# Token-mixing layers in halves of one stream each, set against the FFN of the half before; masks of attn1 on VectorE

## The reference, cut to what matters

```python
def _L1_attn_ref(x, Wqkv, Wo):          # 16 heads of 16
    ...
    scores = jnp.einsum('bhqd,bhkd->bhqk', q, k) / math.sqrt(DH)
    causal = jnp.tril(jnp.ones((t, t), dtype=bool))
    scores = jnp.where(causal, scores, -jnp.inf)
    attn = jax.nn.softmax(scores, axis=-1)
    ...
def _layer(x, wqkv, qs, ksc, wo, lg, lb, w1, b1, w2, b2):   # 8 heads of 64, window 128
    h = shift_token(x)
    q, k, v = jnp.split(h @ wqkv, 3, axis=-1)
    ...
    q = l2norm(q) * qs
    k = l2norm(k) * ksc
    q, k = rotary_xpos(q, k)
    o = local_attention(q, k, v)
    ...
    x = x + o @ wo
    h = shift_token(x)
    ...                                  # layer norm, gain and bias
    h = h @ w1 + b1
    a, g = jnp.split(h, 2, axis=-1)
    h = a * jax.nn.gelu(g, approximate=False)
    x = x + h @ w2 + b2
    return x
x = x + _L1_attn_ref(_layernorm(x, axis=-1), L1_attn_Wqkv, L1_attn_Wo)
x = x + _L1_ffn_ref(_layernorm(x, axis=-1), ...)     # _layer twice
```

## Time and profile before

| what | value |
|---|---|
| median of 3 runs | 2722.84 us (2721.39 to 2726.86) |
| the profiled execution | 2726.97 us |
| its span, first to last instruction | 2725.2 us, 46487 instructions |
| mean granted clock of TensorE | 0.916 |
| attn1 | 598 to 1234 us |
| layers | 1234 to 2725 us |

### The profile page before, as it was taken

How to read it: one execution, slowest core, us unless ns; L and a number is a source line. 1 busy time by engine, 2 the same in 40 slices (tenths; PEclk the granted TensorE clock), 3 DMA queues, 4 the chain that set the end, 5 groups by cost and what they waited for, 6 DMA issues and landing times.

```text
span 2725.2 us, 46487 instructions
## 1 busy us (share of the span) xinstructions
PE 2377.3 (87%) x16770; PEld 1799.0 (66%) x16770; DVE 1564.7 (57%) x4242; ACT 1206.8 (44%) x3055; POOL 965.5 (35%) x1367
## 2 busy tenths in 40 slices
PE   7999699977888888886788898898888988988988
PEld 4666599965464555545567676686676766866766
DVE  5555422225647566546657558567675585585754
ACT  1112133324755555653624636437345354372362
POOL 2222122214443333323715416236155262462442
PEclk9999699987988879788899998998999989989999
DMA  3222311121010100003000000000010000000000
GB/s 123 93 100 97 106 38 36 39 71 32 3 58 7 47 18 33 2 10 111 2 16 16 17 16 1 17 16 33 16 57 16 26 8 32 16 2 32 16 2 32
DMA packets 75794, 96.31 MB, mean 35 GB/s; under 512 B 6141, under 2 KB 68946, under 8 KB 75314
## 3 DMA queue, kind: packets, MB, share of 16 engines
q1 hardware_dynamic: 70642, 81.72, 8.9%
q0 software_dynamic: 3408, 9.31, 1.2%
q10 hardware_dynamic: 1520, 2.31, 0.2%
HBM read 62.51 MB, written 30.28 MB: 34 GB/s over the span
## 4 chain that ended last, share of the span: by engine, by line
PE 30%; DVE 14%; POOL 4%; issue 3%; ACT 2%; DVEq 0%; POOLq 0%; ACTq 0%
PE l_bank L1977 6%; PE l_bank L1978 5%; PE l_bank L1979 5%; PE l_bank L2084 4%; POOL l_probs L1622 3%; DVE l_work L1699 3%; DVE l_ss L1680 2%; PE l_bank L2019 2%; PE l_turned L2037 2%; PE l_bank L2053 2%; DVE l_probs L1697 1%; DVE l_probs L1718 1%; PE l_turned L1977 1%; PE l_turned L1978 1%; PE l_turned L1979 1%
## 5 line engine op out<-in xcount | busy, mean ns | idle before, releaser
L1622 POOL TENSOR_SCALAR l_probs<-l_probs,l_rinv 128x256 f32<-128x256 f32 (+1 forms) x512 | 223.3, 455 | 129.0 <-DVE l_rinv L1723 127.9
L1058 DVE TENSOR_REDUCE c_cnmax<-cbank 128x1 f32<-128x384 f32 (+3 forms) x384 | 206.2, 595 | 108.5 <-PE cbank L1249 89.5
L1896 ACT ACTIVATE l_probs<-l_probs,l_nmax 128x256 f32<-128x256 f32 (+1 forms) x512 | 238.9, 473 | 0.0
L1158 ACT ACTIVATE c_cprobsT<-cbank 128x384 f32<-128x384 f32 (+1 forms) x384 | 180.5, 522 | 97.9 <-PE cbank L1275 97.1
L1718 DVE CUSTOM_DVE_ANT_0 l_probs<-l_bank,mask 128x256 f32<-128x256 f32 (+1 forms) x512 | 169.1, 387 | 37.3 <-PE l_bank L2019 22.8
L1606 POOL TENSOR_TENSOR l_work<-l_work 128x512 f32<-128x512 f32 x64 | 82.7, 1292 | 272.5 <-DVE l_work L1699 271.6
L979 POOL TENSOR_SCALAR_AFFINE_SELECT c_cprobsT<-c_cprobsT 128x256 f32<-128x256 f32 x256 | 99.4, 412 | 165.9 <-ACT c_cprobsT L1158 163.8
L2019 PE MATMUL l_bank<-l_kT,l_flipped 64*128 64x256 f32 (+1 forms) x1024 | 152.6, 420 | 0.0
L1942 ACT ACTIVATE l_v<-l_bank,l_b 128x512 f32<-128x512 f32 (+1 forms) x96 | 66.1, 689 | 193.0 <-PE l_bank L1979 193.0
L718 PE MATMUL h_bank<-m_xsT,m_w1s 128*128 128x128 f32 x1248 | 148.4, 278 | 0.3 <-issue 0.3
L1977 PE MATMUL l_bank<-l_part,l_w_high 128*128 128x512 f32 (+1 forms) x288 | 123.1, 427 | 26.3 <-DVE l_yT L1789 26.3
(11 more groups left out here) (273 smaller groups left out, 6358.5 us busy)
## 6 DMA issues: line engine op xcount, KB each, us to landing
w<-in_W1T SPq DMA_DIRECT2D x8, 1024.0 KB, 8.3
w<-in_W2T SPq DMA_DIRECT2D x8, 1024.0 KB, 11.3
l_came<-y_d SPq DMA_DIRECT2D x16, 512.0 KB, 4.2
ys_d<-m_y SPq DMA_DIRECT2D x39, 128.0 KB, 1.7
xn_d<-a_prods SPq DMA_DIRECT2D x8, 512.0 KB, 3.1
c_came<-x_d SPq DMA_DIRECT2D x8, 512.0 KB, 4.8
y_d<-c_raw SPq DMA_DIRECT2D x8, 512.0 KB, 3.7
y_d<-l_probs SPq DMA_DIRECT2D x8, 512.0 KB, 3.4
```

Source lines behind the costliest of these rows:

```text
L1058: dve.tensor_reduce(nmax[:, c % 2, qt, s, i:i + n], S, AX, ALU.max, negate=True).then_inc(nmax_ready[s], 1)
L1158: act.activation(probsT[s][:, c % 2, i, k0:k0 + w], turned_place(j, s)[:, 0:w], ACT.Exp).then_inc(probs_ready[s], 1)
L1622: pool.tensor_scalar(probs[s][:, held(u), h, 0:n], probs[s][:, held(u), h, 0:n], rinv[s][:, u, h:h + 1], 1.0, ALU.mult, ALU.mult)\
L1896: act.activation(probs[s][:, held(u), h, 0:n], probs[s][:, held(u), h, 0:n], ACT.Exp, bias=nmax[s][:, u, h:h + 1], scale=-1.0, accum_out=r ...
```

## The change

**attn1.** The setup block is gone: its DMAs, the row copies and gathers of POOL and the memsets of DVE stand at the head of the main block, with waits where the data is first used. The mask matmuls on PE are gone; DVE takes the row maximum with one tensor_tensor_reduce per head, which adds a bf16 table `later` (zero, and the mask for the diagonal block) on the way. It writes its unused full result to the last rows of `raw`, and waits for the reduction of the same stream before it.

**layers.** The setup block is gone too: w_qkv is cast and split in six pieces, of which a projection waits for its own; each late weight has its own load and semaphore. The trips are replaced by 16 halves n = 2 * pair + s, one stream each, all eight heads of a stream in eight steps of four heads' score blocks. The attention of half n is written together with the hidden products of half n - 1 (HIDDEN_AT gives them to the eleven slots of the attention), contract(n - 1) with the shift and norm of half n, flip_hn and its splits with the rotations of half n + 1. Probabilities have two buffers, FLIP_LAG is 2, OUT_LAG 3. The PSUM has two score banks, two turned banks, one output bank and three free banks, which q, k and v of the projections share with hidden products. Hidden sums are copied out raw (`take_out`, g by ACT, a by DVE); gelu and gated work from SBUF at the end of the slots, so that the table of ACT changes from exponential to gelu once a half. Gain and bias (L1783) go from DVE to ACT. POOL's bias rows stand in attention steps 1 to 4; the splits of w1 and w2 stand in the steps of the first half of layer one, and of the second and third half of layer two.

```diff
-                        S = score_place("scores", u, s)[:].rearrange("p (h k) -> p h k", h=n)[:, :, 0:(qt + 1) * P]
-                        dve.tensor_reduce(nmax[:, c % 2, qt, s, i:i + n], S, AX, ALU.max, negate=True).then_inc(nmax_ready[s], 1)
+                        wide = (qt + 1) * P
+                        ban = later[:, (NT - 1 - qt):NT, :].rearrange("p a b -> p (a b)")
+                        if pair * UNITS + u:
+                            dve.wait_ge(nmax_ready[s], pair * UNITS + u)
+                        for h in range(n):
+                            last = dve.tensor_tensor_reduce(raw[:, CHUNKS - NS + s, h * 2 * P:h * 2 * P + wide], score_place("scores", u, s)[:, h * 2 * P:h * 2 * P + wide], ban, -1.0, 3e38,
+                                                            ALU.add, ALU.min, nmax[:, c % 2, qt, s, i + h:i + h + 1])
+                        last.then_inc(nmax_ready[s], 1)
...
-                                pe.matmul(score_place("scores", u, s)[:, i * 2 * P:i * 2 * P + wide], qT[s][r, p, qt * P:(qt + 1) * P],
-                                          kT[s][r, p, 0:wide], start=True, stop=False)
-                            for half in range(2):
-                                for s in range(NS):
-                                    h = head(s, c, i0 + i)
-                                    r = slice(64 * (h % 2), 64 * (h % 2) + 64)
-                                    at = i * 2 * P + qt * P
-                                    last = pe.matmul(score_place("scores", u, s)[:, at:at + P], g.mask[r, 3 * half, :], g.mask[r, 3 * half + 2, :],
-                                                     start=False, stop=half == 1)
-                                    if half == 1 and i == n - 1:
-                                        last.then_inc(scores_ready[s], 1)
+                                last = pe.matmul(score_place("scores", u, s)[:, i * 2 * P:i * 2 * P + wide], qT[s][r, p, qt * P:(qt + 1) * P],
+                                                 kT[s][r, p, 0:wide], start=True, stop=True)
+                                if i == n - 1:
+                                    last.then_inc(scores_ready[s], 1)
 
                     def flip_maxima(c):
...
+                for s in range(NS):
+                    pool.tensor_copy(rowb[s][:], g.row_of[:, s * NT:(s + 1) * NT]).then_inc(row_first, 1)
+                pool.wait_ge(row_first, NS)
+                for s in range(NS):
+                    gather(pool, s, 0)
...
+        FLIP_LAG, OUT_LAG, SPAN = 2, 3, 11
+        HIDDEN_AT = ((0, 1), (2, 3), (4, 5), (6,), (7,), (8,), (9,), (10,), (11,), (), ())
...
+        probs = sb("probs", [P, 2, 2, 2, 2 * P])
+        probsT = sb("probsT", [P, 2, 2, 4, P])
...
+        score_bank = [ps(f"score{i}") for i in range(2)]
+        turned_banks = ctx.enter_context(nc.psum_tensor("l_turned", [P, 2, L], F32))
+        turned_bank = [turned_banks[:, a, :] for a in range(2)]
+        out_bank = ps("out")
+        free_bank = [ps(f"free{i}") for i in range(3)]
...
+                    for t in range(NT + 1):
+                        if t < NT:
+                            add(t, 0)
+                        if t:
+                            pool.wait_ge(added[s], pair * (2 * NT) + 2 * t)
+                            pool.wait_ge(inv_ready[s], pair * NT + t)
+                            normalise(pool, s, t - 1, 1).then_inc(k_rotated[s], 1)
+                        if t < NT:
+                            add(t, 1)
...
+                def rotations(n, between):
+                    project(n, 0)
+                    between()
+                    project(n, 1)
+                    flip_qk(n, 0)
+                    project(n, 2)
+                    flip_qk(n, 1)
+                    project(n, 3)
+
...
+                flip_rows(0)
+                rotations(0, lambda: None)
+                for n in range(HALVES + 1):
+                    att, ffn = n < HALVES, n > 0
+                    for p in range(SPAN):
+                        if att and p < 2:
+                            scores(n, p)
+                        if ffn:
+                            for k in HIDDEN_AT[p]:
+                                hidden(n - 1, k)
+                        if att and p < 2:
+                            flip_qk(n, p + 2)
+                        if p == 9 and n + 1 < HALVES:
+                            flip_rows(n + 1)
+                        if att and p >= 2:
+                            if p - FLIP_LAG < STEPS:
+                                flip(n, p - FLIP_LAG)
+                            if p < STEPS:
+                                scores(n, p)
+                            if 0 <= p - OUT_LAG < STEPS:
+                                output(n, p - OUT_LAG)
+                            if p == SPAN - 2:
+                                attended(n, 0)
+                                attended(n, 1)
+                    if att:
+                        attended(n, 2)
+                        attended(n, 3)
+                    if ffn:
+                        contract(n - 1, 0, 1)
+                    if att:
+                        shift(n)
+                    if ffn:
+                        contract(n - 1, 1, NT)
+                    if n + 1 < HALVES:
+                        rotations(n + 1, lambda: flip_hn(n))
+                    elif att:
+                        flip_hn(n)
         nc.all_engine_barrier(sems_to_clear=sem_range)
 
         with nc.Block() as block:
```

More of the change, by code:

```diff
@@ L1419, in phase_layers @@
+        gate = flipped
         kT = stream("kT", [P, HP2, L])
         v = stream("v", [P, NT, INNER])
[L1422 removed]
         hn = [a[:, 2:NT, :].rearrange("p a (b n) -> p (a b) n", n=D) for a in v]
[L1424 to L1430 removed]
@@ L2057, in hidden @@
-                    def hidden(s, c):
-                        if c >= 2:
-                            pe.wait_ge(u_done[s], pair * UC + c - 1)
-                        r = rows(c)
-                        for i in range(2):
-                            for k in range(DC):
-                                last = product(bank[s][2 * (c % 2) + i][0:r, :], [w1[a][:, k, i * HID + c * P:i * HID + c * P + r] for a in (1, 0)],
-                                               [a[:, k, 1:L + 1] for a in (part[s], yT[s])], k == 0, k == DC - 1)
-                        last.then_inc(ag_psum[s], 1)
@@ L2087, in _ @@
-                    for u in range(UNITS + OUT_LAG):
-                        if 0 <= u - FLIP_LAG < UNITS:
-                            flip(u - FLIP_LAG)
-                        if 2 <= u < UNITS:
-                            scores(u)
-                        if u >= OUT_LAG:
-                            output(u - OUT_LAG)
-                        if u == UNITS:
-                            pe.wait_ge(late_in, (layer + 1) * LATE_ALL)
-                        for s in range(NS):
-                            if u >= UNITS:
-                                attended(s, u - UNITS)
@@ new lines, in output @@
+                def output(n, j):
+                    s = place(n)[0]
+                    J = n * STEPS + j
+                    for a in range(2):
+                        pe.wait_ge(pT_ready[a], J + 1)
+                    if j == 0 and n:
+                        f, f_pair = place(n - 1)[0:2]
+                        pe.wait_ge(hn_ready[f], f_pair * (2 * NT) + 2 * NT)
+                    elif j and j % 2 == 0:
+                        pe.wait_ge(oT_ready, J // 2)
+                    cp, w = step_of(j)
+                    k0, width = (w - 1, 2) if w else (0, 1)
+                    for h in range(2):
+                        for k in range(width):
+                            for half in range(2):
+                                head, at = (2 * (2 * cp + h) + half) * DH2, (2 * (j % 2) + h) * P
+                                last = pe.matmul(out_bank[DH2 * half:DH2 * (half + 1), at:at + P], v[s][:, k0 + k, head:head + DH2],
+                                                 probsT[:, j % 2, half, 2 * h + k, :], start=k == 0, stop=k == width - 1, tile_position=(0, DH2 * half))
+                    last.then_inc(pv_done, 1)
@@ new lines, in attended @@
+                def attended(n, t):
+                    s, pair, layer, trip = place(n)
+                    pe.wait_ge(oT_ready, n * (STEPS // 2) + STEPS // 2 - 1 + t // 2)
+                    if t == 0:
+                        pe.wait_ge(wo_in, 16 * (layer + 1))
+                        pe.wait_ge(nmax_ready, 4 * STEPS * (n + 1))
+                    elif t >= 2:
+                        pe.wait_ge(y1_ready[s], pair * NT + t - 1)
+                    for c in range(HP2):
+                        last = pe.matmul(score_bank[t % 2][:, 0:D], oT[s][:, c, t * P:(t + 1) * P], wo[:, c, :], start=c == 0, stop=c == HP2 - 1)
+                    last.then_inc(wo_psum[s], 1)
@@ new lines, in contract @@
+                def contract(n, first, end):
+                    s, pair, layer, _ = place(n)
```

(11 more changed lines are left out.)

1156 lines of the change are left out of this document (618 added, 538 removed).

## The result

The changed kernel takes 2743.06 us (median of 6, 2738.57 to 2750.14) against 2724.86 us before (2721.39 to 2727.57): a ratio of 1.0068, 95% interval 1.0052 to 1.0084, slower by 0.7%. Forecast was 2737. Its profiled execution spans 2745.2 us (forecast 2739.7).

| term | forecast | measured |
|---|---|---|
| first product of the layers | 1233.9 | 1229.4 |
| first half alone | 81.2 | 87.7 |
| PE's work in a half | 77.1 to 77.4 | 79.6 |
| PE's idle time in a half | 13.3 | 10.1 |
| a half at full clock | 90.6 | 89.7 |

A forecast was written before the change was run, and what follows sets the result against it. PE, busy 2377.3 of 2725.2 us, was taken as the bound. 1254.6 - 18.7 - 2.0 + 81.2 + 15 x 91.6 + 44.7 + 3.4 + 2.5 gave a span of 2739.7, so 2737 us; range 2665 to 2800.

The forecast's parts named there:

- PE's work in a half: Layers: projections, hidden products, attention steps, wo, contract, flips and shift sum to 77.1 us; the trace gave 77.4.
- PE's idle time in a half: Layers: PE waits 13.3 us per half, from rotations 5.0, attention steps 3.5 and the end of a half 4.8.
- the fill: First half of the layers, with no FFN to fill it: 81.2 us from first to second first-projection.
- the drain: End of the layers: last FFN without attention 44.7 us, store and end 3.4; with the last half, 139.7.
- attn1's gain: attn1: mask matmuls leaving PE give -15 us (from -28 to 0), the setup block's removal -3.7; 18.7 together.
- Rotations: Projection turns of one half run alone: a lap takes 7.7 us against 5.2 of PE work; two open laps add 5.0.
- Attention steps: Attention with hidden chunks: the loop is covered but for 0.3 us; starts and the single output bank make +3.5 together.
- The end: End of a half: flip(7) waits 1.8 us, output(6) 1.5, attended(2) 1.5; +4.8 in the sum.
- The clock: Term: half clock adds 1.0 us per half. Rival: waits keep it at 0.50 longer, P = 95.5, 2795 us; chance 0.16.
- The extras of the second layer's weights: Halves in which the second layer's weights are split: 2.5 us extra, from 0 to 9.
- Faster, PE near its work: Layers, rival: waits at step ends overlap and full clock holds; P = 87.5 us per half, 2676 total; chance 0.36.
- the masked reduction: attn1, rival: DVE's reduction waits for itself and becomes the bound; attn1 gains 0, sum 2752; no chance of its own.

The follow-up runs named there:

- POOL's order: Changed kernel with POOL normalising k of the turn before ahead of adding q of the next turn in the rotations: 2718.31 us, ratio 0.9985 to the kernel before.
- the turns: Changed kernel with POOL, DVE and ACT each finishing rotation turn t-1 before starting turn t: 2667.70 us, ratio 0.9795 to the kernel before.
- the output first: Changed kernel with ACT's copy of the attention output placed ahead of its copy of the turned probabilities: 2710.61 us, ratio 0.9947 to the kernel before.
- both orders: Changed kernel with rotation turns finished in order on three engines and ACT's attention output copied out first: 2648.17 us, ratio 0.9732 to the kernel before.

## Why the prediction was right, point by point

In short: the direction, the cause of the loss and the length of a half came out as forecast. That the total is only 6 us off in 2740 is in part luck: in the half, in the fill and in the drain, errors of 2 to 14 us have opposite signs.

**The balance.** It named the reason of the small loss: attn1's gain against fill and drain, with a half about as long as before (91.3 against 90.6). Attn1 gave 21 us (forecast 18.7 for the stage), some 14 of them the mask (forecast 15; 16 by the medians, 8 to 11 by the stage's length in the profiles). The layers took it back, and as much again. Their first product came 4.5 us earlier than forecast, which hides most of the error in the fill.

**The half.** 90.6 was forecast at full clock and 89.7 measured, but two errors cancel in it. PE's work was put 2.2 us too low. For the order of before, 77.4 was right: the stretches at 0.50 of its trip, 13.7 and 6.8 us long, hold 15.2 us of PE's busy time, so the half clock adds 3.8 a half ("about 4") and leaves 77.6. The step that failed is that the new order would keep this work because it "removes no matmul". It has as many (590 a half) and is busy 79.6. By the distance from each matmul's start to the next (or to its own end where PE then waits), in one half at full clock, hidden products take 18.6 us (forecast 16.8), the attention's matmuls 19.7 (18.5), projections 17.7 (16.8), and flips of q and k 3.3 (4.2). A hidden product alone between other kinds, and what comes next:

```profile
1724.90 0.50 PE L2072 MATMUL l_free<-l_part,l_w_high 128*128 128x512 f32 x1
1726.50 0.71 PE L2166 MATMUL l_turned<-ident,l_probs 64*128 64x64 f32 x16
```

It takes 1.60 us, where 1.40 was read from an unbroken row of them. Idle time was put 3.2 too high. *Rotations*: the lap was the right place and its cause half right. 5.0 was forecast, 3.7 measured. The lap is 7.1 us, where 7.7 was forecast. The first flip waits 1.85, where 2.5 was said, and its releaser is not POOL's normalise but DVE's of q, which the lock holds beside POOL's add; I had costed the lock at 0.7 a lap, and it is 0.95 (1.64 less 0.69). With the lock gone and the add out of the way (POOL's order) a half gained only 1.3, as DVE's turn still stood ahead of its inversion. *Attention steps*: 3.5 forecast; 1.1 for the row maximum and 0.7 for the output bank came true, hidden's wait was 0.4, the flip's 0.2: about 2.4. A step is 3.76 us (1722.75 to 1726.50), where 4.0 was forecast. *The end*: 4.8 forecast, 1.35 + 1.27 + 1.42 = 4.0 measured, at the three waits named.

**The clock.** 1.0 forecast, 1.6 measured, 0.2 of it from the second half, which is at full clock. The clock falls in two places, in the laps of the rotations (11 to 13 us after a half's first product) and at the end of the attention (68 to 70 us after it), each time for 3.4 or 6.8 us, though no wait of PE is over 1.9 us. In halves at 89.7 and at 92.9 PE waits in the same places. The waits that a fall covers or follows are shorter (residual 0.7 in place of 1.4, the second lap's flip 0.7 in place of 1.3), the others are the same to 0.1 us, so nothing in PE's waits tells the two apart. What decides stays open. Nor do shorter waits make the falls rarer in every case. In the twelve plain halves of a profile, 48 us are at 0.50 in the changed kernel, 41 with POOL's order, 17 with the turns, 24 with the output first, and 37 with both orders, whose waits are the shortest of these. The same layers in the kernel with the mask on PE have 34, so one execution's figure can differ by 14 from another's, and only the turns' 17 is further than that from both.

**Fill and drain.** The drain's total was right to a microsecond, by two errors: after the fifteenth half the clock is at 0.50 for 26 us, which adds 8 us to PE's busy time where the sum has 1.0, and PE is idle for 26 us, where the sum leaves some 35. The fill was 6.5 us too low in the same way: PE is at 0.50 for 36 of the first half's 87.7 us, which adds 14.3 us to its work of 50.1 (forecast 50.5), and it is idle 23.3 us, where the term leaves 30.7. My term took a half near full clock as its basis. The extras of the second layer's weights were 9.7 against 2.5. The bound of 9 was there (190.0 less 181.2), but 2.5 was taken without a row, and without what DVE has beside the split: two-operand instructions, at the end of a half on which PE waits. The lock was known from the earlier trace rows; the step that failed was to apply it to the rotations alone. The half of layer two's w1 has 6.8 us more of PE's wait for the residual, and 10.2 us at 0.50.

**The lock and the rule.** The Trainium skill, SBUF — State Buffer, section "Who interferes with whom", says that the one cause of contention is a pair of ports that DVE and GpSimd share under an exclusive lock, and that issue order decides who blocks. The runs agree: gated started 0.39 us after the subtraction of 6.27 us, took 6.43 and ended 0.55 us after it; and normalise at 1641 ns beside the add and at 693 once the add came later. They add what a reader should know of long instructions: in pieces, the two engines alternate.

**The rivals.** "The clock": eight halves were longer than the 89.7 at full clock, seven of them with a fall, but the mean of 91.3 stayed under the 91.6 forecast. "Faster, PE near its work" did not happen in this kernel, and it did with two lines of order changed on each of three engines: 86.2 us a half in the mean, below its bound of 87.5. I had put the lap down as a property of one half running alone, "which nothing fills". It was a property of the order within the lap. In attn1 the masked reduction did not become the bound; the chunk of 8.54 us is just over the 8.3 to 8.5 that were said.

## What to carry to other kernels

When two streams that ran side by side are taken apart, each queue's order has to be read again: an instruction for turn t that stood harmlessly ahead of one for turn t-1 becomes the loop. Matmuls of different kinds set between each other can take longer than each kind in a row, though none is added: here 2 us a half. Write out, for each lap, which engine's order forces the next product before the last result; here that was 75 us, four times the loss that the change brought. And price a long two-operand instruction on POOL by what DVE has to do beside it, not by POOL's own load.

## What the runs showed of the hardware

- An instruction of DVE with two SBUF operands, issued 0.39 us after a POOL subtraction of 6.27 us, took 6.43 us in place of 0.74. With POOL's work in four pieces, three of DVE's took 2.11 to 2.12 us each and POOL's pieces 2.04, against 6.27 / 4 = 1.57.
- The masked row maximum of attn1, whose scores come from PSUM and whose mask is the only SBUF operand, takes 687 ns for 512 columns, as long as the plain reduction of before (684 ns). But it is one per head, and a read of the accumulator of 83 ns follows each, so DVE's row maxima are busy 219 us in all, where they were 206.
- A product of six matmuls of 512 columns took 1.60 us of PE between matmuls of other kinds, against 1.40 in a row of like ones (0.70 for three).
- Halves of the same program, with waits of PE in the same places and none over 1.9 us, took 89.7 or 93.0 us: the granted clock was 1.00 throughout, or 0.50 for 10.2 us.
